# Four chained transformer blocks on one core: the last block's output product in two parts, with new turns and PSUM places

## The reference

```python
xn = _layernorm(x, axis=-1)
x = x + _L3_attn_ref(xn, ...) + _L3_ffn_ref(xn, ...)

def _L3_attn_ref(...):   # 16 heads of 16 channels
    attn = softmax(scores, axis=-1)
    out = einsum('bgqts,bgsd->bgqtd', attn, v).transpose(...).reshape(b, s, HID)
    return out @ Wo.T + bo

def _L3_ffn_ref(...):    # 8 experts, the best 2 of them weighted, and a shared one
    shared_out = jax.nn.sigmoid(g) * u @ shared_down.T
    comb = zeros.at[rows, top_idx].add(top_w)
    he = jax.nn.sigmoid(ge) * ue
    de = einsum('nei,ehi->neh', he, wd)
    routed = (comb[:, :, None] * de).sum(axis=1)
    return x + shared_out + routed
```

## Time and profile before

| | us |
|---|---|
| runs (three) | 1212.25, 1212.69, 1215.65 |
| profiled execution: its time | 1219.58 |
| profiled execution: span of its instructions | 1218.0 |
| PE busy | 1096.1 (90%) |
| DVE busy | 841.0 (69%) |
| ACT busy | 641.5 (53%) |
| POOL busy | 498.2 (41%) |
| mean granted clock of PE | 0.951 |

### The profile page before, as it was taken

How to read it: one execution, slowest core, us unless ns; L and a number is a source line. 1 busy time by engine, 2 the same in 40 slices (tenths; PEclk the granted TensorE clock), 3 DMA queues, 4 the chain that set the end, 5 groups by cost and what they waited for, 6 DMA issues and landing times.

```text
span 1218.0 us, 17428 instructions
## 1 busy us (share of the span) xinstructions
PE 1096.1 (90%) x6542; PEld 720.0 (59%) x6556; DVE 841.0 (69%) x1602; ACT 641.5 (53%) x980; POOL 498.2 (41%) x549
## 2 busy tenths in 40 slices
PE   3698999999999888999579999999699998997998
PEld 2466686766665454674257998989234543553445
DVE  6985856678568897955767435267877679668751
ACT  6644647466569885642135333242187166465473
POOL 4864748375524526411774052244231331141131
PEclk9778999999999999998789999999799989998999
DMA  7724344324340101267370000006914526425320
GB/s 216 214 55 146 87 129 149 116 79 142 94 174 35 36 1 48 70 198 229 106 75 27 1 1 1 1 10 159 217 38 122 140 55 149 101 67 155 92 72 18
DMA packets 86116, 116.42 MB, mean 96 GB/s; under 512 B 29617, under 2 KB 43281, under 8 KB 85265
## 3 DMA queue, kind: packets, MB, share of 16 engines
q1 hardware_dynamic: 47792, 70.28, 19.2%
q0 software_dynamic: 38240, 45.03, 15.1%
HBM read 81.54 MB, written 40.40 MB: 100 GB/s over the span
## 4 chain that ended last, share of the span: by engine, by line
PE 61%; DVE 14%; ACT 7%; POOL 6%; issue 6%; DMA 5%; SPq 1%; ACTq 0%; DVEq 0%; POOLq 0%
PE pair L693 23%; PE bank L693 18%; PE bank L772 6%; PE pair L762 5%; PE pair L751 4%; DVE max L1157 3%; POOL gathered L2092 2%; ACT probs L1681 2%; DMA h<-comb 1%; PE pair L712 1%; PE bank L780 1%; SPq L2124 1%; POOL h L2110 1%; PE pair L792 1%; DMA kept<-q_low 1%
## 5 line engine op out<-in xcount | busy, mean ns | idle before, releaser
L1157 DVE TENSOR_REDUCE max<-pair 128x2 f32<-128x1024 f32 (+3 forms) x256 | 252.5, 1021 | 61.7 <-PE pair L742 32.1
L1681 ACT ACTIVATE probs<-pair 128x1024 f32<-128x1024 f32 (+3 forms) x256 | 212.5, 865 | 103.3 <-PE pair L762 85.6
L751 PE MATMUL pair<-ks,qs 64*128 64x512 f32 (+3 forms) x512 | 110.6, 456 | 24.4 <-DVE max L1157 10.8
L2013 POOL TENSOR_TENSOR h_low<-hidden,h_high 128x512 fp32r<-128x512 f32 x64 | 82.8, 1299 | 97.8 <-ACT h_high L1719 97.3
L772 PE MATMUL bank<-probs,v 128*32 128x512 f32 (+3 forms) x1024 | 115.4, 536 | 1.1 <-POOL probs L2057 0.5
L762 PE MATMUL pair<-qs,ks 64*128 64x512 f32 (+3 forms) x512 | 102.1, 435 | 13.3 <-DVE max L1157 5.1
L751 PEld LDWEIGHTS pair<-ks,qs 64*128 64x128 f32 x512 | 50.4, 199 | 80.3 <-DVE max L1157 31.5
L762 PEld LDWEIGHTS pair<-qs,ks 64*128 64x128 f32 x512 | 46.2, 190 | 76.7 <-ACT probs L1681 24.5
L1713 ACT ACTIVATE hidden<-pair 128x512 f32<-128x512 f32 x64 | 38.2, 599 | 80.9 <-PE pair L693 69.9
L2110 POOL TENSOR_TENSOR h<-mix_h,h 128x512 bf16<-128x512 f32 x48 | 54.9, 1172 | 57.4 <-DMA h<-comb 39.1
L1196 DVE TENSOR_TENSOR x<-bank,x 128x512 f32<-128x512 f32 x32 | 22.0, 688 | 80.2 <-PE bank L693 80.1
(11 more groups left out here) (330 smaller groups left out, 2673.9 us busy)
## 6 DMA issues: line engine op xcount, KB each, us to landing
kept<-q_high SPq DMA_DIRECT2D x64, 256.0 KB, 3.8
qs<-kept POOLq DMA_DIRECT2D x32, 512.0 KB, 4.1
ks<-kept POOLq DMA_DIRECT2D x32, 512.0 KB, 5.2
kept<-q_low SPq DMA_DIRECT2D x32, 256.0 KB, 4.1
expert_in<-in_experts_in SPq DMA_DIRECT2D x16, 352.0 KB, 4.1
expert_out<-in_experts_out SPq DMA_DIRECT2D x16, 256.0 KB, 5.5
h<-comb SPq DMA_DIRECT2D x4, 1024.0 KB, 5.5
tern_raw<-in_ffn_in SPq DMA_DIRECT2D x8, 256.0 KB, 6.6
```

The costliest lines, as they stand in the source:

```text
L751: made = mm(to[:, hh, 0:n], m.qs[k][slot][r0:r0 + STACK, p, qt * P:(qt + 1) * P], m.ks[k][slot][r0:r0 + STACK, p, 0:n], start=True, stop=k ...
L1157: V.tensor_reduce(m.max[:, g % 2, :, p, qt], to[:, :, 0:n], AX.X, ALU.max).then_inc(*s.done("top"))
L1681: A.activation(m.probs[(2 * kt + p) % 4][:, :, q0:T], to[:, :, q0:T], ACT.Exp, scale=0.25).then_inc(*s.done("exp"))
L2013: Q.tensor_tensor(m.h_low[k][:, j, :], m.hidden[k][j % 2][:, :], m.h_high[k][:, j, :].bitcast(F32), ALU.subtract).then_inc(*s.done("low"))
```

## The change

In the last block the output product becomes two parts. "out" keeps only the attention's product, `rowsT` by `wo`. A new PE part, "blend", one for each batch and half, sums the shared expert's product and the experts' product in a bank of its own; a new DVE part, "blended", adds that bank to x. So x gets two additions for each half instead of one. Of each such pair the one that has the later turn waits for the other. `comb_load` and the ACT part that writes `shared_h` now wait for the blends, "store" for both additions. The tables `DUE` and `TAKEN` are written anew for the whole kernel. Most of the new numbers swap neighbours.

```diff
-        "back": keys(HEADS, B, range(G)), "rows": keys((0, 1, 3), B), "out": keys(ALL, B, PAIRS),
+        "back": keys(HEADS, B, range(G)), "rows": keys((0, 1, 3), B), "out": keys(ALL, B, PAIRS), "blend": keys(B, PAIRS),
...
-    "rows": "138 253 349 426 465 489 498 526 784 911 1025 1095",
-    "out": "142 141 255 259 365 374 429 428 474 472 493 492 514 513 535 536 610 611 627 625 650 647 673 674 788 792 918 922 1035 1031 1096 1097",
+    "rows": "138 253 349 426 466 489 498 525 784 911 1030 1100",
+    "out": "141 143 255 259 369 374 428 429 476 470 493 492 514 513 535 536 610 611 628 625 650 648 674 672 789 797 915 923 1036 1035 1102 1104",
+    "blend": "786 793 919 927 1044 1040 1103 1105",
...
-        if k == 3:
-            pe.wait_ge(*at("half", k))
-        if k in (1, 3):
+        if k == 1:
             pe.wait_ge(*at("shared_out", k, b, 0))
             pe.wait_ge(*at("shared_out", k, b, 1))
-        if k == 3:
-            pe.wait_ge(*s.experts3_landed())
-            pe.wait_ge(*s.last("mix_comb", [(b, j) for j in range(MIX)]))
...
-            if k in (1, 3):
-                made = products(to[:, cols], [(m.shared_h[k][b % 2][:, c, tok], m.shared_w[k][:, c, :]) for c in PAIRS], start=False, stop=k == 1)
-            if k == 3:
-                made = products(to[:, cols], [(m.h16[:, j, tok], m.w16_out[:, j, :]) for j in range(MIX)], start=False)
+            if k == 1:
+                made = products(to[:, cols], [(m.shared_h[1][b % 2][:, c, tok], m.shared_w[1][:, c, :]) for c in PAIRS], start=False)
         made.then_inc(*s.done("out"))
+
+    def blend(b, i):
+        to = bank("blend", b, i)
+        pe.wait_ge(*at("half", 3))
+        pe.wait_ge(*at("shared_out", 3, b, 0))
+        pe.wait_ge(*at("shared_out", 3, b, 1))
+        pe.wait_ge(*s.experts3_landed())
+        pe.wait_ge(*s.last("mix_comb", [(b, j) for j in range(MIX)]))
+        for n in PAIRS:
+            tok, cols = slice((2 * i + n) * P, (2 * i + n + 1) * P), slice(n * C, (n + 1) * C)
+            products(to[:, cols], [(m.shared_h[3][b % 2][:, c, tok], m.shared_w[3][:, c, :]) for c in PAIRS], stop=False)
+            made = products(to[:, cols], [(m.h16[:, j, tok], m.w16_out[:, j, :]) for j in range(MIX)], start=False)
+        made.then_inc(*s.done("blend"))
...
+        if k == 3 and s.turns.before(("blended", (b, i)), ("joined", (k, b, i))):
+            dve.wait_ge(*at("blended", b, i))
         V.tensor_tensor(x_pair(b, i), to[:, :].rearrange("p (t c) -> p t c", t=2), x_pair(b, i), ALU.add).then_inc(*s.done("joined"))
+
+    def blended(b, i):
+        to = bank("blend", b, i)
+        dve.wait_ge(*at("blend", b, i))
+        dve.wait_ge(*at("with_xn", b))
+        if s.turns.before(("joined", (3, b, i)), ("blended", (b, i))):
+            dve.wait_ge(*at("joined", 3, b, i))
+        V.tensor_tensor(x_pair(b, i), to[:, :].rearrange("p (t c) -> p t c", t=2), x_pair(b, i), ALU.add).then_inc(*s.done("blended"))
...
-        sp.wait_ge(*s.last("out", [(3, b - 1, i) for i in PAIRS] if b else [(2, b2, i) for b2 in B for i in PAIRS]))
+        sp.wait_ge(*(s.last("blend", [(b - 1, i) for i in PAIRS]) if b else s.last("out", [(2, b2, i) for b2 in B for i in PAIRS])))
```

More of the change, by code:

```diff
@@ L818, in out @@
             else:
-                made = products(to[:, cols], [(m.rowsT[k][:, kc, tok], m.wo[k][:, kc, :]) for kc in range(KC)], stop=k == 0)
+                made = products(to[:, cols], [(m.rowsT[k][:, kc, tok], m.wo[k][:, kc, :]) for kc in range(KC)], stop=k != 1)
             if k == 2:
@@ L1022, in mix @@
         made.then_inc(*s.done("mix"))
[L1024 removed]
+    parts = {"tern_sum": tern_sum, "turn": turn_x, "qk": qk, "vals": vals, "score": score, "prob": prob, "weigh": weigh, "back": back, "rows": rows, "out": out, "blend": blend,
              "unit": unit, "down": down, "mean": mean, "proj": proj, "gate": gate, "gamma": gamma, "inflow_turn": inflow_turn, "mem_turn": mem_turn, "shared": shared,
@@ L1813, in shared_tanh @@
         elif b > 0:
-            act.wait_ge(*s.last("out", [(3, b - 1, i) for i in PAIRS]))
+            act.wait_ge(*s.last("blend", [(b - 1, i) for i in PAIRS]))
         else:
```

76 lines of the change are left out of this document (39 added, 37 removed), and 275 rows, old and new, of the table DUE.

## The result

| | kernel before | changed kernel |
|---|---|---|
| median of the runs side by side, us | 1214.17 (four, 1212.25 to 1217.32) | 1230.74 (four, 1228.02 to 1232.97) |
| ratio, 95% interval | | 1.0114, 1.0078 to 1.0151 |
| profiled execution, span, us | 1218.0 | 1230.8 |

The change makes the kernel slower, by 1.1% or some 14 us (the two medians stand 16.6 us apart). The changed kernel was timed twice more beside the kernel before, on other chips: 1.0102 (1.0056 to 1.0148) and 1.0164 (1.0109 to 1.0218). 1230.7 us lies outside the range of 1201 to 1217. Three executions of the kernel before in later groups, of 1762, 2594 and 3521 us, were slow ones and are left out of every ratio.

The account below looks back on a forecast made before the run. PE was taken to set the pace in the last block; -2.0 -1.5 -0.4 +0.5 -1.1 -0.6 = -5.1 us gave 1214.5 profiled, 1207.6 us as median of runs. Range 1201 to 1217 us.

Parts of the forecast that it names:

- What bounds the kernel: Last block: PE, busy 328.36 of 368 us, sets the pace; gains only where it idles or its clock is low.
- The split itself: Last block: six added DVE additions, 4.1 us, cost nothing because they lie where DVE stands idle.
- DVE becomes the bound: Rival, last block: DVE's idle time no longer covers the six additions; +4.2 us, 1216.9 us; chance 0.20.
- Batch 0: After batch 0's output products: earlier broadcast of expert weights lets POOL start sooner; -2.0 us waiting, -1.5 us clock.
- The first term: 959 to 972 us: PE's 2.34 us of waiting mostly go; -2.0 us, between -3.2 and 0.
- The second term: 979 to 986 us: PE's clock may stay up without holes; -1.5 us, between -3.1 and 0.
- Batch 1: Batch 1's output products: broadcast +0.3 us later, but PE meets DVE less late; -0.4 us.
- Batch 2: Batch 2's output products: broadcast 1.2 us later, first h product behind the maxima's transfer; +0.5 us.
- The rest of the table: Whole kernel, other turns: swaps of neighbours in nearly every engine's order cost nothing, plus or minus 2 us.
- The end: Last output: shared product covers ACT's copy of the turned rows, PE's 1.10 us hole goes; -1.1 us.
- The gathers: Join of second and third block: POOL's gathers start 2.0 us earlier, less 1.4 for a product; -0.6 us.
- The signs: Listed trace marks for right (h products before 965, gathers by 587, DVE waits under 2.5 us) or wrong (later batch 3 broadcast).

Follow-up runs that it names:

- order_only: Changed kernel's new turns and PSUM places without the split, the last block's output product again one accumulation; 1252.2 us, 1.0291 of the kernel before.
- before_again: The kernel before, unchanged, profiled again on another chip; 1216.5 us.
- bl1: Changed kernel with, in batch 1 alone, both blends ahead of both attention products; 1.0041 of the kernel before.
- b_max: Changed kernel with POOL's fetch of one head group's maxima (3,2,2) moved back behind batch 2's h products; 1.0013 of the kernel before.
- a_act: Changed kernel with ACT's copy combT of batch 2 moved ahead of three probs activations; 0.9991 of the kernel before.
- c_pool: Changed kernel with POOL's gathers of (3,3,1) moved back behind its fetch of the maxima (3,2,3); 1.0001, later 1.0121 of the kernel before.
- c_both: Changed kernel with POOL's gathers (3,3,1) back behind the maxima's fetch and SP's batch 3 comb store back ahead of the keeps; profiled once, PE's wait 0.30 us, not 6.99.

## Why the prediction was wrong

*What bounds the kernel.* PE sets the pace on average, but the reading stopped one step short. Where PE waited, I asked what the change did to that wait; I didn't ask at which places a chain of transfers was only just in time, and what the new order puts ahead of its links. In the first trace PE already waited 1.10 us for maxima at the first place.

*The split itself: nothing.* Not contradicted: no wait of PE in the last block of the changed kernel is for one of DVE's adds, and order_only, which has none of them, loses the same at all three places. But no run takes the adds out alone. The rival "DVE becomes the bound" had the sign of the result by another mechanism. The rule of the Trainium skill (Trainium Kernel Development and Optimization, Best Practices) that tiling TensorE's work does not speed up the emptying of PSUM did not decide here: DVE waited 13.7 and 3.2 us for the two kinds of output product in the last block, where it had waited 29.1. It was fed no better for that: its waits for score tiles grew from 28.1 to 40.2 us, so that both together are the same, 57 us.

*Batch 0: -2.0 for PE's holes, -1.5 for the clock.* The first term is right: the h products start at 963.68 (the mark was 965), PE is busy 19.68 of 20 us from 950 to 970 at full clock, and from 940 to 975 each of the three traces of the changed kernel gains 2.4 us, where the four of the old order have 0.0, 0.0, -0.2 and +0.3. The second term was a fault of the reading: from 975 to 1000 the changed kernel gains 0.8 to 1.2, and the old order 0, 2.7, 1.4 and 2.7. In before_again the clock is 1.00 from 970 to 990, where I read 0.53 in the one trace that has 0. So the change's own gain is nearer 1.7 us (4.8 less the mean of 0, 3.2, 4.1 and 5.0); that the step of -4.8 looks like the forecast is luck.

*Batch 1: -0.4, between -0.7 and +0.5.* **This step failed in size.** The later broadcast, put at +0.3 us, was 1.0 us later than PE, then slower, and held the maxima too: +4.8 for the step. bl1, which sends it earlier, takes 3.0 back. POOL's gathers come right ahead of the broadcast; I priced the wait for the broadcast, not what shares the DMA engines with it. And POOL's fetch of the maxima moved ahead of the h products here, a swap that I didn't cost: b_max, which moves it back, takes 2.6.

*Batch 2: +0.5, between 0 and +2.4.* A little too dear: -0.1 to -0.4 in the stretch to 1180.

*The rest of the table: nothing, plus or minus 2.* **This step failed outright**, and carries most: +3.5 at the first place (a_act takes 4.0 back) and +7.6 at the third (c_pool takes 2.7 back, and c_both removes the wait for the maxima). "Swaps of neighbours" was true, but a swap of one bring with one max_bring on POOL and one of a store with the keeps on SP put 7 us of waiting where I had set nothing. I listed POOL's and SP's queues only where the split touched them.

*The end: -1.1, between -1.5 and 0.* The hole for rowsT is gone as forecast: wo follows the shared product at once.

```profile
1210.43 1.06 PE L796 MATMUL pair<-ident_r,heads 128*128 128x128 f32 x8
...
1213.88 0.39 PE L697 MATMUL pair<-cut_low,shared_in_high 128*128 128x512 f32 x1
1214.12 1.89 PE L697 MATMUL bank<-wo,rowsT 128*128 128x256 f32 x8
```

But the stretch is +0.3 to +0.6, not -1.1: another hole, 0.71 us for probs, opened ahead of it, and the last mix turn moved in.

*The gathers: -0.6, between -1.8 and +1.4.* Inside its range, but the gain isn't there. They start at 587.99, short of the mark of 587, and the first turn of block 2 is at 612.74 instead of 613.00; but at 580 us this trace is already 1.1 us ahead of the first one. By the pairing the three traces of the changed kernel lose 0.8 to 1.0 us from 580 to 613, those of the old order -0.2 to +0.2: the gathers start no earlier in step, and the root behind them is later. At 850 us sixteen traces with the new turns stand at -3.9 to +3.4, mean 0.0, four with the old at 0 to 10.0, mean 4.2. So blocks 0 to 2 as a whole show no loss; whether they gain is not settled by four.

*The signs.* Of those named as right, two failed: DVE waits 2.96 us for an output product before the end (2.5 was the mark), and the gathers start after 587. Of those named as wrong one came true by the letter: the broadcast of batch 3 leaves at 1174.31 and not at 1160.82. But PE is itself 12.5 us late by then, so this is what the three places left, and not a cause. No sign looked at the transfers of the maxima behind batch 0, where the time was lost.

Open is the rest of the third place, 0.7 to 1.7 us from 1112 to 1118 in the three traces of the changed kernel, where PE waits longer for the keys (2.95 instead of 1.58 us); no edit took that wait away. What the clock alone costs behind each hole wasn't tried apart.

## What to carry to other kernels

When a table of turns is made anew, walk each queue that carries a small transfer someone waits for (here 16 KB of maxima on SP and POOL), and write down what stands right ahead of it and right behind it, on both queues, before and after. Here one group's gathers moved ahead cost the small send 2 us, where their own two issues take 1.4. Where a step ends earlier, look whether the next chain of transfers starts earlier with it, and count the gain only if it does: at the first place it did in before_again and did not in the changed kernel. And read a low clock in a single trace as a price only if a second trace shows it.

## What was not expected of the hardware

The time from SP's issue of the same 16 KB to POOL's fetch depends on what else is in flight. At the third place it was 2.8 us in before, 4.7 in c_pool and 6.7 in the changed kernel (one or two groups' gathers). At the second place, behind the 1 MB broadcast, it was 5.4, 7.0 and 7.4 us in the three traces of the changed kernel and 7.4 in a_act, and 2.9 in bl1, where the broadcast had left 10 us ahead of the maxima. The Trainium skill (DMA: Bandwidth & Descriptors, Queues, rings and completion order) says that a DMA engine serves its queues in turn, a packet of each; by that a small transfer of SP is slowed by POOL's bulk but need not wait for its end. The traces agree: the slowing is up to 2.6 times (7.4 against 2.8), and in the changed kernel the maxima issued at 1119.92 landed after 6.4 us, while the keys' gather that POOL had issued before them, at 1119.34, took 9.5:

```profile
ks<-kept POOLq DMA_DIRECT2D x1, 512.0 KB, 9.5
kept_max<-max_rows SPq DMA_DIRECT2D x1, 16.0 KB, 6.4
```

The 1.8 us that c_both leaves of the send coincide with a third kind of traffic. A packet of 16 KB on the queue that the profile calls "instruction" starts at 1118.37 and takes 0.97 us; ahead of it the gather and the maxima are through but for the last few packets, and these go only between 1119.3 and 1119.9. In the kernel before that packet has 8 KB and takes 0.31 us. All sixteen traces with the new turns have the larger one 2.1 to 3.0 us behind the issue of these maxima, the four with the old turns the smaller one. No run moved it, so that it makes the 1.8 us is likely and not shown.

SP took 3.3 us to issue the broadcast in a_act, b_max and two of the three traces of the changed kernel, 2.2 in the other, and 1.6 in before and in bl1; what decides between 2.2 and 3.3 is open.

The kernel before took 1214, 1225, 1217, 1224, 1217 and 1225 us in the median of six groups of runs on different chips, while the changed kernel took 1230.7, 1230.0 and 1233.1 in three, and c_pool, timed in two groups, gave 1.0001 and 1.0121: ratios of edits from different groups can differ by a percent with nothing changed.
